# Two of the eight kv multiplications of the first half go from GpSimd to VectorE, in a newly ranked order of steps

## The reference, cut to what matters

```python
kv = jnp.einsum('bhil,bhjl->bijhl', k_, v_)
kv_f = jnp.fft.rfft(kv, n=fft_size)
kernel_f = jnp.fft.rfft(ssm_kernel, n=fft_size)
y = jnp.fft.irfft(kv_f * kernel_f, n=fft_size)[..., :L]
out = y + kv * D[None, None, None, :, None]
out = jnp.einsum('bijhl,bhil->bjhl', out, q_)
...
x = x + jnp.tanh(g_xattn[0]) * _L0_xattn_ref(ctx_2048, ctx_2048, _layernorm(x, axis=-1), L0_xattn_ssm_kernel, L0_xattn_D, 8)
x = x + jnp.tanh(g_ffn[0]) * _L0_ffn_ref(_layernorm(x, axis=-1), L0_ffn_gate_w, L0_ffn_mask_up_w, L0_ffn_gate_proj_w, L0_ffn_up_proj_w, L0_ffn_down_proj_w, L0_ffn_inv_map)
x = x + jnp.tanh(g_xattn[1]) * _L1_xattn_ref(_layernorm(x, axis=-1), ctx_2048, mask_BxS2_bk0)
x = x + jnp.tanh(g_ffn[1]) * _L1_ffn_ref(_layernorm(x, axis=-1), L1_ffn_w_fc, L1_ffn_w_proj)
```

## Time and profile before

| | |
|---|---|
| median of 3 timed runs | 234.39 us (234.38 to 235.89) |
| span of the profiled execution | 233.6 us, first to last instruction; it is the one figure that this profile gives for its own time |
| PE busy | 222.1 us (95%) |
| PEld busy | 214.4 us (92%) |
| DVE busy | 176.0 us (75%) |
| ACT busy | 111.2 us (48%) |
| POOL busy | 83.6 us (36%) |
| granted PE clock | 0.998 of full |
| HBM traffic | 10.14 MB read, 1.07 MB written |

### The profile page before, as it was taken

One profiled execution on the slowest core, in us unless ns is written; L12 is line 12 of the kernel. 1 busy time (PEld: TensorE's weight loads), 2 busy tenths in 40 slices (PEclk: granted clock), 3 DMA queues, 4 the chain that ended last, 5 costly groups with the idle time before them and its releaser, 6 DMA issues.

```text
span 233.6 us, 4695 instructions
## 1 busy us (share of the span) xinstructions
PE 222.1 (95%) x1600; PEld 214.4 (92%) x1600; DVE 176.0 (75%) x494; ACT 111.2 (48%) x231; POOL 83.6 (36%) x143
## 2 busy tenths in 40 slices
PE   6899789989999999999999999999999999999994
PEld 5899787879999999999999999999999999988883
DVE  4277979998999999789977697743777566555874
ACT  2233257932444450654364464748724772335443
POOL 4569997656647631100503433002022102010520
PEclk9999999999999999999999999999999999999999
DMA  6699864000000001500000000000000100010011
GB/s 181 164 356 222 260 210 130 1 0 3 0 1 3 0 3 22 203 4 0 0 3 0 0 3 1 4 0 0 3 0 0 39 9 3 0 46 0 4 46 45
DMA packets 14055, 11.51 MB, mean 49 GB/s; under 512 B 2928, under 2 KB 13776, under 8 KB 14032
## 3 DMA queue, kind: packets, MB, share of 16 engines
q1 hardware_dynamic: 13936, 11.16, 15.9%
q10 hardware_dynamic: 96, 0.05, 0.1%
HBM read 10.14 MB, written 1.07 MB: 48 GB/s over the span
## 4 chain that ended last, share of the span: by engine, by line
PE 75%; DVE 7%; SPq 6%; DMA 6%; issue 2%; ACT 2%; POOL 1%; ACTq 0%; DVEq 0%; POOLq 0%
PE bank L758 26%; PE bank L596 14%; PE bank L603 11%; PE bank L761 4%; PE bank L829 4%; DMA ring<-in_up_p 4%; PE bank L813 3%; PE bank L647 2%; PE bank L649 2%; PE bank L648 2%; PE bank L799 1%; SPq L552 1%; SPq L561 1%; PE bank L787 1%; DMA lags<-in_kernel_rev 1%
## 5 line engine op out<-in xcount | busy, mean ns | idle before, releaser
L758 PE MATMUL bank<-w_split,xt 128*128 128x352 f32 x384 | 69.0, 328 | 0.2 <-issue 0.2
L758 PEld LDWEIGHTS bank<-w_split,xt 128*128 128x128 f32 x384 | 61.0, 188 | 0.4 <-issue 0.4
L1256 DVE SCALAR_TENSOR_TENSOR act<-silu,scal,bank 128x176 f32<-128x176 f32 x64 | 22.6, 393 | 19.2 <-ACT silu L961 19.0
L596 PE MATMUL bank<-d_split,a_t 128*128 128x256 f32 x264 | 33.4, 285 | 0.0
L596 PEld LDWEIGHTS bank<-d_split,a_t 128*128 128x128 f32 x264 | 32.2, 192 | 0.0
L961 ACT ACTIVATE silu<-bank 128x352 f32<-128x352 f32 x32 | 14.9, 465 | 33.5 <-PE bank L761 33.4
L1414 POOL TENSOR_TENSOR fold<-prod 128x256 f32<-128x256 f32 x32 | 23.7, 742 | 9.7 <-DVE att L1113 6.5
L1403 POOL TENSOR_TENSOR kv<-ctx_ext 128x640 f32<-128x640 f32 x16 | 20.0, 1254 | 6.5 <-PE bank L649 3.9
L838 ACT ACTIVATE a_t<-bank 128x384 fp32r<-128x384 f32 (+1 forms) x32 | 14.8, 461 | 13.5 <-PE bank L603 13.4
L1354 POOL TENSOR_SCALAR ve<-mv 128x2 f32<-128x2 f32 (+2 forms) x11 | 3.0, 276 | 44.9 <-DVE mv L1049 44.9
L1016 DVE TENSOR_TENSOR a_t<-bank,a_t 128x384 fp32r<-128x384 f32 (+1 forms) x32 | 16.6, 518 | 2.8 <-ACT a_t L838 2.8
(11 more groups left out here) (151 smaller groups left out, 451.8 us busy)
## 6 DMA issues: line engine op xcount, KB each, us to landing
toe<-lag_rows SPq DMA_DIRECT2D x4, 512.0 KB, 7.7
ring<-in_down_p SPq DMA_DIRECT2D x2, 704.0 KB, 4.6
ctx<-in_ctx_rows SPq DMA_DIRECT2D x2, 512.0 KB, 5.0
ring<-in_gate_p SPq DMA_DIRECT2D x2, 512.0 KB, 6.8
ring<-in_up_p SPq DMA_DIRECT2D x2, 512.0 KB, 8.8
out_x<-x_res SPq DMA_DIRECT2D x3, 256.0 KB, 2.1
tern_w<-in_w_fc SPq DMA_DIRECT2D x1, 640.0 KB, 4.3
tern_w<-in_w_proj SPq DMA_DIRECT2D x1, 640.0 KB, 5.5
```

The costliest lines, as they stand in the source:

```text
L596: last = pe.matmul(dst, lhs(a), rhs(b), start=start and i == 0, stop=stop and i == 2)
L758: pe.matmul(psum((name, b, c))[:, 0:CW], lhs, w_split[:, w, kt, part, cols], start=i == 0, stop=False)
L1256: drain(dve.scalar_tensor_tensor(out=act[:, g * NI:(g + 1) * NI], in0=silu[:, n % 2, cols], scalar=scal[:, b, g:g + 1], in1=psum(("up", b, ...
```

## The change

Groups 2 and 4 of the first half (`KV_BY_DVE`) are multiplied by DVE, with the same instruction on the same operands (now L499 in a helper `make_kv`). A second semaphore, `kv_beside`, counts them; PE waits for it in these groups and for `kv_made` in the others. All numbers of `TIMES` are replaced; they are now plain ranks. The number of matmuls on constants stays the same (KEEPS and WARMS are not touched).

```diff
--- before.py
+++ after.py
@@ -48,6 +48,7 @@
 DONE_TILES = [range(0, 2), range(2, 5), range(5, 8), range(8, 11)]
 WORDS = {"gate": 0, "up": 1}
 TERNARY = ["fc", "proj"]
+KV_BY_DVE = [(0, 2), (0, 4)]
 UNITS = [range(0, 2), range(2, 4), range(4, 6), range(6, 7), range(7, 8)]
 
 
@@ -64,44 +65,43 @@
...
-    "kv0": [-5075, -4713, -3031, -2795, -1719, -1529],
...
-    "gather0": [-2997, -2342, -1641, -1322, -1109, -1029, -471, -366],
...
-    "keeps": [-4795, -3979, 143, 143, 153, 196, 260, 2008],
...
+    "kv0": [15, 25, 32, 33, 41, 50],
...
+    "gather0": [28, 29, 46, 53, 60, 68, 75, 76],
...
+    "keeps": [11, 12, 106, 107, 117, 118, 127, 351],
...
@@ -437,7 +437,7 @@
     mix_made = sem("mix_made")
     mu4_cleared = sem("mu4_cleared")
     mu4_made, onehot_made, ind_made = sem("mu4_made"), sem("onehot_made"), sem("ind_made")
-    kv_made = sem("kv_made")
+    kv_made, kv_beside = sem("kv_made"), sem("kv_beside")
     prod_cleared, summed = sem("prod_cleared"), sem("summed")
     folded, gathered = sem("folded"), sem("gathered")
     gain_made, scale_made = sem("gain_made"), sem("scale_made")
@@ -483,6 +483,21 @@
 
     def group_no(half, g):
         return half * (HEADS // 2) + g
+
+    def pool_kvs(half, g):
+
+        return sum(divmod(n, HEADS // 2) not in KV_BY_DVE for n in range(group_no(half, g) + 1))
+
+    def make_kv(eng, half, g):
+
+        n = group_no(half, g)
+        if n >= 2:
+            hf, gg = divmod(n - 2, HEADS // 2)
+            for h in (2 * gg, 2 * gg + 1):
+                wait_filled(eng, ("conv", hf, h))
+        base = (half * HEADS + 2 * g) * 2 * Q * EXT
+        return eng.tensor_tensor(kv[:, n % 2], view(ctx_ext, base, [[EXT, 4 * Q], [0, TAPS], [1, HD]]),
+                                 view(ctx_ext, base, [[EXT, 4 * Q], [1, TAPS], [1, HD]]), ALU.mult)
 
     def view(t, offset, dims):
 
@@ -637,7 +652,10 @@
                     g = group_no(half, h // 2)
                     if half == 0:
                         pe.wait_ge(toe_loaded[h // 4], 16)
-                    pe.wait_ge(kv_made, g + 1)
+                    if (half, h // 2) in KV_BY_DVE:
+                        pe.wait_ge(kv_beside, KV_BY_DVE.index((half, h // 2)) + 1)
+                    else:
+                        pe.wait_ge(kv_made, pool_kvs(half, h // 2))
                     claim(pe, step)
 
                     def pairs(t):
@@ -1103,6 +1121,11 @@
                                         [[ROWS * HD, 2 * Q], [HD + 1, 3], [1, HD]])
                     drain(dve.tensor_tensor(shifted_rows, view(y, HD, [[YW, 2 * Q], [HD, 3], [1, HD]]),
                                             view(q_ext, qb, [[EXT, 2 * Q], [0, 3], [1, HD]]), ALU.mult), step)
+                elif kind == "kv" and step[1:] in KV_BY_DVE:
+                    _, half, g = step
+                    for t in range(2):
+                        wait_drained(dve, ("turn_ctx", half, t))
+                    make_kv(dve, half, g).then_inc(kv_beside, 1)
                 elif kind == "gather":
                     _, half, g = step
                     n = group_no(half, g)
@@ -1389,20 +1412,12 @@
                     pool.wait_ge(scale_made, 1)
                     pool.tensor_scalar(gain[:, u, 0:n], late[:, 1, u, 0:n], out_scale[:, 2:3], None,
                                        ALU.mult).then_inc(gain_made, 1)
-                elif kind == "kv":
+                elif kind == "kv" and step[1:] not in KV_BY_DVE:
                     _, half, g = step
-                    n = group_no(half, g)
                     if g == 0:
                         for t in range(2):
                             wait_drained(pool, ("turn_ctx", half, t))
-                    if n >= 2:
-                        hf, gg = divmod(n - 2, HEADS // 2)
-                        for h in (2 * gg, 2 * gg + 1):
-                            wait_filled(pool, ("conv", hf, h))
-                    base = (half * HEADS + 2 * g) * 2 * Q * EXT
-                    pool.tensor_tensor(kv[:, n % 2], view(ctx_ext, base, [[EXT, 4 * Q], [0, TAPS], [1, HD]]),
-                                       view(ctx_ext, base, [[EXT, 4 * Q], [1, TAPS], [1, HD]]),
-                                       ALU.mult).then_inc(kv_made, 1)
+                    make_kv(pool, half, g).then_inc(kv_made, 1)
                 elif kind == "fold":
                     _, half, h = step
                     n = group_no(half, h // 2)
```

More of the change, by code:

```diff
@@ L66 @@
 TIMES = {
[L67 to L71 removed]
[11 rows of a table removed]
[L83 to L90 removed]
[14 rows of a table removed]
+    "weights": [22, 23, 24, 40, 42, 49, 56, 61, 62, 63, 70, 73, 74, 77, 78, 81, 83, 84, 86, 92, 97, 105, 122, 136,
+        137, 138, 150],
+    "lows": [80, 82, 85, 89, 91, 93, 98, 101],
+    "consts": [57],
+    "onehot": [96],
[10 rows of a table added]
+    "mask": [221],
+    "ternary": [197, 202, 209, 224, 225, 233, 238, 245, 246, 249, 258, 261, 272, 275],
+    "chunks": [149, 151, 161, 171, 181, 183, 190, 194, 198, 203, 205, 213, 217, 222, 228, 229, 236, 240, 253, 255,
+        260, 264, 273, 276, 281, 294, 295, 298, 303, 309, 318, 324],
+    "turns": [157, 170, 180, 185, 189, 196, 200, 207, 212, 216, 218, 226, 231, 235, 237, 241, 244, 252, 259, 265,
+        268, 271, 279, 285, 293, 297, 302, 308, 313, 319, 322, 327],
+    "downs": [187, 210, 230, 243, 267, 288, 314, 330],
+    "keeps": [11, 12, 106, 107, 117, 118, 127, 351],
[14 rows of a table added]
 }
```

12 lines of the change are left out of this document (removed), and 45 rows, old and new, of the table TIMES.

## The result

The changed kernel takes 237.28 us (median of 4 runs, 236.32 to 238.95), the kernel before 234.39 us in the runs beside it. The medians lie 2.9 us apart. The ratio on record, which is not that of the two medians, is 1.0103, with a 95% interval of 1.0064 to 1.0143: about 2.4 us slower. The forecast was 233.9 us with a range to 236.2; the time lies outside it, on the other side of the old one. The ratios leave out slow runs, those over 1.5% above the fastest of the same kernel, and of all the runs here this takes out only three of e4.

The account below looks back on a forecast made before the run. PE was taken as nearly full, with DVE the bound from 31.45 to 56 us. The terms, 0.15 - 0.6 + 0 + 0 = -0.45 us, took the median 234.39 to 233.9 us, range 232.2 to 236.2.

Parts of the forecast that it names:

- The bound: Whole kernel: PE, busy 222.1 of 233.6 us, can gain little more than its waits; POOL's saved 2.5 us is worth nothing.
- The two multiplications on DVE: Between 13 and 31 us: 822 ns each, 1.64 us together, up to 3.1 us if held by POOL's folds; one hold counted.
- Term 1: DVE's work up to the first `up` weights at 31.45 us ends 0.15 us late: +0.15 us, between 0 and +1.5.
- 0.6 us late or more: Sign at DVE's remainder of the first `up` weights, expected at 31.4 to 31.7 us: this lateness would mean the forecast is wrong.
- Term 2: End of the first half, around the first router: earlier norm, shorter integer instruction, statistics moved away; -0.6 us, between -0.3 and -0.7.
- The transfer waits: The two `up` loads: the first stays fixed on SyncE's queue, the second is issued later but used later too; 0 us.
- Term 4: From 61.5 us on: same PE matmuls and unchanged shortest distance between dependent steps; 0 us, between -0.3 and +1.
- The new list opens a wait later: Rival: from 100 us on, a copy or remainder later than its reader costs 0.5 to 2 us; 235.2 us, chance 0.11.
- slow DVE: Rival: holds against POOL and the late start make DVE late at the first `up` remainder; 235.5 to 236.9 us, chance 0.18.
- the waits of PE go: Rival: DVE gets ahead, PE's 1.2 and 0.7 us waits vanish and three fillers are saved, 2.6 us; 231.8 us, chance 0.14.

Follow-up runs that it names:

- e4: The changed kernel's list up to the first chunk, the order of before behind it, kv multiplications on DVE as in the change; 235.27 us, ratio 0.9971.
- e1: The kernel before, its order kept, with only the kv multiplications of groups 2 and 4 moved to DVE; 235.51 us, ratio 1.001.
- e2: The changed kernel's new order with all eight kv multiplications left on POOL; 237.82 us, ratio 1.0099.
- e4 again: The same kernel as e4, timed a second time; 235.67 us, ratio 1.0028.
- e9: e4 with seven matmuls on constants added ahead of the first `up` transposition, in a bank long free; 235.1 us, ratio 1.0009.
- e10: The changed kernel with seven matmuls on constants added ahead of the first `up` transposition, in a bank long free; 237.15 us, ratio 1.0062.
- e3: The changed kernel with seven matmuls on constants moved from ahead of the first convolution to ahead of the first `up` transposition; 238.95 us, ratio 1.0149.
- e5: The kernel before up to its first chunk, then the changed kernel's list, both kv multiplications on DVE; 237.96 us, ratio 1.0089.
- e7: The changed kernel's list up to `chunk 4 0`, from there the order of before; 236.25 us, ratio 1.0046.
- e8: The changed kernel with three places as before: `turn_a 2 2`, `turn_a 7 0` and all that follows `down 7`; 236.43 us, ratio 1.0037.
- e12: The changed kernel with DVE's norm `cross 0` moved behind the remainder of `turn_a 2 1`; 237.68 us, ratio 1.0111.
- e14: e12 with DVE's norm `mlp 2` also moved, behind the remainder of `turn_a 6 3`; 235.74 us, ratio 1.0051.

## Why the prediction was wrong, point by point

**The bound: right.** PE's idle time decides, and POOL's relief was worth nothing (e1: 1.001). The chain still runs through the first `up` load.

**The two multiplications on DVE: right in price, wrong in who pays.** They took 0.83 and 0.81 us, the estimate was 0.82. In the changed kernel neither was held, as one was expected to be. POOL's fold was held in its place, at both:

```profile
14.00 0.83 DVE L499 TENSOR_TENSOR kv<-ctx_ext 128x640 f32<-128x640 f32 x1
```

```profile
14.02 1.40 POOL L1429 TENSOR_TENSOR fold<-prod 128x256 f32<-128x256 f32 x1 [2.16 <-DVE prod L1122]
...
21.20 1.26 POOL L1429 TENSOR_TENSOR fold<-prod 128x256 f32<-128x256 f32 x1
```

The fold's mean before is 742 ns. Started 0.02 us behind DVE it took 1.40; in e1 DVE started 0.01 us behind POOL's fold and was the one held. The Trainium skill, "SBUF — State Buffer", section "Who interferes with whom", has it so: the later one is blocked in full. The traces agree in who is held, in both directions, and nearly in how long: the fold at 14.02 took 0.66 us more where 0.81 of the multiplication was left, that of e1 on DVE 0.58 more where 0.73 of the fold was left.

**Term 1, +0.15 us: the account held only for one kind of start.** The first product was to start at 15.0 us. In e2, which has this order and no kv on DVE, it starts there, and in the changed kernel 1.8 us earlier:

```profile
15.00 0.49 DVE L1117 TENSOR_TENSOR prod<-bank,q_ext 128x320 f32<-128x320 f32 x1 [1.68 <-PE bank L667]
```

```profile
13.19 0.49 DVE L1117 TENSOR_TENSOR prod<-bank,q_ext 128x320 f32<-128x320 f32 x1 [1.68 <-PE bank L667]
```

The cause stands ahead of it on PE. The same seven matmuls on constants (14 rows), with the same code in front of them, before and after:

```profile
8.50 2.94 PE L612 MATMUL bank<-ident,ones 128*128 128x128 f32 x14
```

```profile
7.84 1.73 PE L627 MATMUL bank<-ident,ones 128*128 128x128 f32 x14
```

This differs by execution, not by kernel: the same code of e4 took 1.73 us in one profile and 2.27 in the other. It is 2.94 us in before, e1 and e2, 2.27 to 2.39 in e4 again, e9 and e10, 1.73 in the changed kernel, e3, e4, e5, e7, e8, e12 and e14. The first product of those with the new order and its full start comes at 15.00, at 14.34 to 14.45, and at 12.92 to 13.19. So in this execution DVE was early, not 0.15 us late, PE reached the end of the work ahead of the `up` load sooner, and all that this brought was a longer wait. DVE's remainder of the `up` weights started at 32.12 in place of 31.45, having waited 1.83 us for ACT:

```profile
32.12 0.69 DVE L1034 TENSOR_TENSOR w_split<-bank,w_split 128x512 fp32r<-128x512 f32 x1 [1.83 <-ACT w_split L856]
```

The transposition ahead of it, four rows, ran at half clock (1.11 us busy, against 0.66 at full clock in e7, where the remainder starts at 31.60 behind a load at 30.27). By the prediction's sign, "0.6 us late or more", this was to be read as a slow DVE. It was not: 0.23 of the 0.67 us is the later load (30.35 for 30.12), 0.44 the way from the load to the remainder, which is PE's clock by the comparison with e7.

**Term 2, -0.6 us: right in kind, too large.** The integer instruction fell from 1.28 to 0.20 us, since POOL's kv multiplication is no longer beside it:

```profile
47.11 0.20 DVE L1048 TENSOR_SCALAR inv_i<-inv_i 64x64 int32<-64x64 int32 x1
```

The norm wait ahead of the first router is gone in the changed kernel (0.6 us of it are left in e2), and a wait of 0.3 us stands ahead of the top-8 transposition, for which up to 0.7 was expected. But from the first `up` transposition to the first chunk it takes 32.75 us at best (e8: 29.04 to 61.79) against 32.97 before: 0.2 us. It takes 33.11 in e4 again, 33.29 to 33.34 in e4, e7, e9 and e12, in which PE waits another 0.40 to 0.47 us for an `up` load near 32 us, and 33.95 in the changed kernel with the half clock.

**The transfer waits, 0: failed in part.** The first chunk moved with the landing of the first `up` load. It was turned between 28.64 and 30.49 us in the kernels with the new front, whose code up to there is the same but for the fill. And the later `up` load, which I had set to cost nothing, was late by those 0.40 to 0.47 us in four of them. Over the seven new fronts without an added fill the first chunk stands at 62.98 us in the mean, over the three old ones at 63.18. With the ratios (e4 at 0.9971 and 1.0028) the front comes to nothing that can be measured, where I had -0.45 us.

**Term 4, 0: this is the step that failed.** It measured +1.94 us (+2.3 like against like), beyond its own upper end of 1. I had compared "the PE work between each `chunk` and its `turn_a`, and between products that share banks". The reader of the one bank that all `turn_a` share is a DVE instruction, and its place is in DVE's queue. The distance that mattered is from one `turn_a` to the next, less what stands in DVE's queue ahead of the first one's remainder. Before, `turn_0 0` and `flat 2` stood on PE between `chunk 3 0` and `turn_a 2 2`, and the norm was finished long ahead:

```profile
112.19 0.62 DVE L1068 TENSOR_SCALAR xn<-x_res,mv 128x256 f32<-128x256 f32 x2
112.99 0.70 DVE L1256 SCALAR_TENSOR_TENSOR act<-silu,scal,bank 128x176 f32<-128x176 f32 x2 [0.18 <-ACT silu L961]
113.61 0.55 DVE L1016 TENSOR_TENSOR a_t<-bank,a_t 128x384 fp32r<-128x384 f32 x1
```

The new list took the work away on PE and put the norm ahead of the remainder on DVE. That this is the cause at the two places is shown: moving the norms alone gave back 0.63 + 0.54 = 1.17 us of the back (e12, e14), about half of the loss. The rest, 0.8 to 1.1 us, is not explained.

**What stays open.** After e14 the back is 168.73, 0.8 us over the kernel before (1.1 over e4). Against before, 0.64 us of this is PE's busy time and 0.15 idle time, at full clock and with the same number of rows: the list of waits cannot show where it is. By e7 against e4 the larger part of the loss lies ahead of `chunk 4 0`. One piece there has the same form: the remainder of `turn_a 2 0` stands behind the statistics of `cross 0`, and the next turning starts 0.46 us behind the two transpositions ahead of it, where before the same kind of pair follows in 0.22 (109.68 to 109.90). Most of these 0.24 us are inside the busy time: the row at 113.73 ends at 114.11, and a pause of 0.08 us is below what the list shows.

```profile
112.70 0.75 DVE L1064 BATCH_NORM_STATS2 stats<-x_res 128x6 f32<-128x256 f32 x2
113.49 0.25 DVE L1067 BATCH_NORM_AGGREGATE mv<-stats 128x2 f32<-128x6 f32 x2
113.66 0.39 DVE L1034 TENSOR_TENSOR a_t<-bank,a_t 128x256 fp32r<-128x256 f32 x1
```

```profile
113.73 0.38 PE L618 MATMUL bank<-ident,rt 128*64 128x128 f32 x2
114.19 0.52 PE L618 MATMUL bank<-ident,act 128*128 128x128 f32 x3
```

This was argued, not tried. The last units are no part of the loss, though their waits changed (0.67 for a norm and 0.9 for `hid_t` after, others before). The last `turn_a` starts 146.38 us behind the first chunk before, 146.03 in e4, 148.53 in the changed kernel and 147.36 in e14, each time with 150 rows of matmuls still to run, and from there to the last `x_res` it takes 21.56, 21.57, 21.35 and 21.37 us: the new order gains 0.2 us there. Nor is it settled what share of the changed kernel's 2.4 us beyond the back's 1.94 is chance in the loads and what is the half clock.

**The rivals and the chances.** "The new list opens a wait later" named the mechanism, a remainder later than its reader, and had 0.11 and 0.5 to 2 us; the back took 1.9. It deserved more: the trace shows PE at 20.00 of 20.00 us, so there PE had nothing to gain from any reordering and every changed place could only lose. The "slow DVE" did not come, nor did "the waits of PE go": the norm and the product left the list, and a longer wait for the load took their place. The base was a little low too: the changed kernel's runs lie 1.8 us above their spans, so the 233.6 us span of before belongs to a run of about 235.4, not to the median 234.39 that I had set it against.

## What to carry to other kernels

When a reordering touches a stretch in which the bounding engine is full, list for each shared buffer its last reader and what stands ahead of that reader in the reader's own queue; comparing distances on the bounding engine alone misses this. Compare its busy time as well as its waits: 0.6 to 0.8 us of the loss here was in no wait. Where a bank has one copy, put long instructions that nobody waits for behind its release, not ahead of it. A part of a program that ends in a fixed transfer varies with that transfer: read the two parts from marks in the trace, because a gain of 0.6 us in one is hidden in the whole time by the other.

## What the runs showed of the hardware

The granted clock of PE fell to half (1.2 in place of 2.4 GHz) in or just after idle times of 2.35 us (changed), 2.36 (e3) and 2.23 (e5), and did not with 2.34 (e7), 2.57 (e12) and 2.26 (e14): the same idle time gives both, so a wait of this length puts the next microseconds at risk and no more. Matmuls on constants cover such a wait only in a bank that is free; in e3 they inherited the wait of their bank and made it worse. At the start of the program the same 14 rows of matmuls took between 1.73 and 2.94 us; the granted clock reads 1.00 from 7 to 11 us in the profile of the changed kernel (1.73) as in that of the kernel before (2.94), so the profile doesn't call this the clock. The ratio of the durations, 1.7, is that of the transposition rows at half and at full clock near 30 us (1.11 and 0.66), so it may be the clock all the same; no run here settles it. It moves the first product by up to 2 us, and the `up` load swallows it.

DVE and POOL hold each other in both directions, the later one for nearly the whole rest of the earlier: 1.40 for 0.74 us on POOL, 1.41 for 0.83 us on DVE, held for 0.15 us less than the rest of the other in both cases.
